# A two-layer graph network on one core: fillers at norm 2 and in attention's last pair, single heads, a 15th unit before the experts, GpSimd adds, and another order in relation 1

## The chip, the cores and the metric

The kernel runs on one core of a Trainium2 chip. The metric is the device time of one execution in microseconds (us). Five sequencers work at once: PE (TensorE, matrix products), DVE (VectorE), ACT (ScalarE), POOL (GpSimd) and SP (SyncE, which here issues the weights' DMAs). They wait for one another only by semaphores, and each takes its instructions strictly in the order in which the program lists them.

## The reference

There are 625 nodes of D = 1024 float32 features and 10,625 edges. Cut to what matters:

```python
xn = layernorm(x)
x = x + gnn0(xn) + mix0(xn)         # support[src]*w summed by dst; linear attention
x = x + ffn0(layernorm(x))          # 16 experts, top 2, capacity 98, F=1408, and a shared MLP
xn = layernorm(x)
x = x + gnn1(xn) + mix1(xn)
x = x + ffn1(layernorm(x))          # 8 small experts, a shared MLP

def ffn0(x):
    probs = softmax(x @ router_w + router_b); vals, idx = top_k(probs, 2)
    # each expert gets its rows (at most 98), mlp(h) = silu(h@wg)*(h@wu) @ wd
    return x + mlp(x, sw_gate, sw_up, sw_down) + gathered.reshape(N, 2, d).sum(1)

def gnn1(x):                        # u: relations r = 0..7
    u = x @ root + bias + sum_r mean_r(x[src] -> dst) @ weight[r]
    z = concat([u, x]) @ w_gate + b_gate
    return tanh(u) * z + x * (1 - z)

def mix1(x):                        # 16 heads of 64, 256 features
    q, k, v = split(x @ Wqkv + bqkv)
    f = lambda t: exp(t @ omega - 0.5 * sum(t*t))
    out = f(q) @ (f(k).T @ v) / (f(q) @ sum(f(k)) + 1e-6)
    return out @ Wout + bout
```

## The kernel before

**Tiles and products.** Nodes lie in T = 5 tiles of TP = 125. To keep float32's precision each operand is split in a high part (a copy to fp32r, on ACT, `a_high`) and a low part (the operand minus the high part, on DVE, `v_low` and `lo_of`, line 270), and each product is three matrix products, high by high, low by high, high by low (`mm3`, line 234). TensorE is therefore fed by two steps on two engines: a weight comes by SP's DMA in a raw tile, ACT makes the high part, DVE the low one.

**Order.** No scheduler sets the order. For each engine a program is written out (`tensor`, `scalar`, `vector`, `gpsimd`, `sync`), made of functions with the prefixes t_, a_, v_, p_ and s_ for the five. What must be in the same order on several engines (the weights' chunks) is in a list `W` that `weights` fills; PSUM's eight banks are given out in turn by `ps.take`, and a product waits for the step that emptied its bank.

**Stages** (us in the profiled execution): norm 1, features and linear attention mix0 to 200; the adjacency matrix and its spread to 314 (`t_adjacency`, `t_spread`); norm 2 to about 327; the experts to 1330; norm 3 to 1344; the relations to 1816; attention to 2060; the window to about 2290; then gate, norm 4 and the small ffn.

**Norm 2.** `v_spread` adds the aggregated products to x and takes statistics; tiles 0 to 2 are normalized and turned (transposed on TensorE, `t_turn_norm`, line 1236) during the spread, tiles 3 and 4 after it in `t_layernorm`. A turned tile leaves PSUM as T_h by ACT (`a_turned_norm`) and T_l by DVE (`v_turned_norm`). The space of T is shared, and `T_free` says from when it may be written. Then comes routing: `t_route` makes the logits from rw, in two halves of the nodes.

**Experts.** The shared MLP is cut into units (`t_unit`: a gate, an up or a down block, about 7 us of TensorE each), 11 during routing, three more before the experts, and then one with each of experts 0 to 10 and with expert 15. Ten indirect DMAs of POOL (`scr_ei<-xn,sdi`, line 2228) scatter the rows to the experts' places; `xin<-scr_ei` reads one expert's back, and `t_enter` transposes them. At the end ten gathers bring the experts' outputs yg back, and `v_combine` weights and adds two of them for each tile on DVE, among the last units; `v_add_x` adds the last units' products, with the statistics of norm 3.

**Relations.** Each relation's product is made in blocks by sums and differences of quarters of the matrix B and of T (`v_block_mixed`, `v_mixed`, and their low parts `v_block_low`). `v_last` makes one more of the sums.

**Attention.** Eight pairs of heads. For a pair p, z (k or q, `v_z`) is split in both heads at once, then `t_keys`, `t_queries`, `t_values`, `t_turn_values` and `t_attend` follow for s = 0, 1; features are made by ACT and split by DVE (kp, qp); kw is the product of keys and values, rt the divisor, whose reciprocal `v_over` takes 628 columns.

**Window.** 200 slots in five blocks of 40 (KD = 8 chunks of k by T = 5 tiles): root and Wout in two halves each, then one block of the gate. A slot is one `mm3`. Between slots SUM0 = 14 and SUM1 = 178 lie the 96 sums of gathered rows (`t_sum`): for each, POOL gathers 128 rows of y (`gr`, line 2345), ACT scales them (`gh`, line 2308) and makes a 0/1 matrix (`gs`), DVE makes the low part (`gl`, line 266), TensorE makes four products, and the buffers (six) come free for another gather. `a_part` and `v_part` split the attention's output oT into oh and ol in the first block.

## Time and profile before

| | us |
|---|---|
| three runs: lowest, median, highest | 2518.45, 2518.72, 2530.13 |
| the profiled execution, its own time | 2521.97 |
| its span, first to last instruction | 2520.1 |
| TensorE busy | 2438.6 (97%) |
| DVE busy | 1811.3 (72%) |
| ACT busy | 1421.7 (56%) |
| POOL busy | 653.3 (26%) |
| chain that ended last | PE 84%, DVE 8%, DMA 3%, issue 2%, ACT 2%, POOL 1% |
| mean granted TensorE clock | 0.989 of full speed |

A share of busy time is a mean over stages with different limits, so an edit is read at its place: what TensorE waits for there, and what stands ahead of it on the engine waited for. DMA-issuing instructions aren't counted as busy. In timelines a row may be several instructions of one kind ("x16"), with the time that TensorE stood ahead of it and what ended that in brackets.

### The profile page before, as it was taken

The numbers are of one execution on the slowest core, as the hardware profiler recorded it, in microseconds if no ns is written. First come the engines' busy times: TensorE is split into PE (matmuls) and PEld (weight loads), VectorE is DVE, ScalarE is ACT, GpSimd is POOL, SyncE is SP. The second block draws the span as 40 slices with busy tenths as digits, with TensorE's granted clock in tenths as the row PEclk, the third lists the DMA queues.
The fourth block names the chain that finished last, engine by engine and source line by source line (L and its number), as shares of the span: only waits on it lengthen the run. The fifth ranks groups of instructions, "written<-read, shape, count | busy, mean of one in ns | idle before, by whom it ended". The sixth has DMA issues, their size and how long they took to land.

```text
span 2520.1 us, 32144 instructions
## 1 busy us (share of the span) xinstructions
PE 2438.6 (97%) x12692; PEld 2019.6 (80%) x12692; DVE 1811.3 (72%) x2006; ACT 1421.7 (56%) x1890; POOL 653.3 (26%) x538
## 2 busy tenths in 40 slices
PE   7999998999999999999998999999999979999999
PEld 6978788777777777777787777777899977777797
DVE  7449664888878888788868876556567778887453
ACT  5327432777677767777733344443377758884131
POOL 5758204434431000000021005442000016556000
PEclk9999999999999999999999999999999999999999
DMA  6334026999999899999974344445211138884212
GB/s 176 78 100 129 1 80 216 332 337 334 350 352 350 336 335 336 360 390 374 354 216 158 104 155 137 118 135 162 91 44 56 54 114 277 285 275 142 92 56 74
DMA packets 128013, 508.14 MB, mean 202 GB/s; under 512 B 26892, under 2 KB 44697, under 8 KB 101240
## 3 DMA queue, kind: packets, MB, share of 16 engines
q1 hardware_dynamic: 78440, 418.00, 46.2%
q0 software_dynamic: 34928, 74.92, 10.5%
q10 hardware_dynamic: 14496, 13.17, 1.6%
q8 instruction: 101, 1.65, 0.3%
q14 instruction: 48, 0.39, 0.0%
HBM read 458.93 MB, written 46.88 MB: 201 GB/s over the span
## 4 chain that ended last, share of the span: by engine, by line
PE 84%; DVE 8%; DMA 3%; issue 2%; ACT 2%; POOL 1%; SPq 0%; DVEq 0%; ACTq 0%
PE ps L231 83%; DVE od L262 2%; DMA scr_ei<-xn,sdi 1%; DVE Aw L258 1%; DVE x L258 1%; DMA wk<-in_Wk 1%; DVE ua L258 1%; PE ps L2025 1%; PE ps L1236 1%; DMA gr<-scr_y,gidx 1%; POOL scr_ei L2228 1%; DVE zq_l L270 0%; PE ps L1993 0%; DVE ws_l L270 0%; ACT gh L2308 0%
## 5 line engine op out<-in xcount | busy, mean ns | idle before, releaser
L270 DVE TENSOR_TENSOR pr_l<-pr,hs 128x1408 fp32r<-128x1408 f32 (+1 forms) x455 | 645.5, 1444 | 137.3 <-ACT hs L793 134.5
L793 ACT ACTIVATE hs<-pr 128x1408 fp32r<-128x1408 f32 (+1 forms) x455 | 559.0, 1242 | 205.3 <-PE ps L231 164.5
L793 ACT ACTIVATE ws_h<-wr 128x1024 fp32r<-128x1024 f32 (+1 forms) x105 | 110.2, 1051 | 206.7 <-PE ps L231 199.6
L270 DVE TENSOR_TENSOR ws_l<-wr,ws_h 128x1024 fp32r<-128x1024 f32 (+1 forms) x103 | 129.8, 1261 | 115.4 <-ACT ws_h L793 115.2
L231 PE MATMUL ps<-hs,xe_h 128*98 128x512 f32 (+1 forms) x768 | 205.5, 376 | 0.0
L231 PE MATMUL ps<-pr_l,xe_h 128*98 128x512 f32 (+1 forms) x768 | 205.0, 375 | 0.0
L231 PE MATMUL ps<-hs,xe_l 128*98 128x512 f32 (+1 forms) x768 | 204.6, 374 | 0.0
L2234 POOL DMA_DIRECT2D xin<-scr_ei x16 | 9.4, 590 | 581.1 <-PE ps L1993 550.3
L231 PEld LDWEIGHTS ps<-pr_l,xe_h 128*98 128x98 f32 x768 | 124.8, 163 | 38.8 <-DVE pr_l L270 0.9
L231 PEld LDWEIGHTS ps<-hs,xe_l 128*98 128x98 f32 x768 | 125.0, 163 | 38.2
L231 PEld LDWEIGHTS ps<-hs,xe_h 128*98 128x98 f32 x768 | 123.8, 163 | 36.7
L2345 POOL DMA_INDIRECT gr<-scr_y,gidx x96 | 125.0, 1302 | 100.2 <-PE ps L231 78.9
L3058 POOL DMA_INDIRECT wrow<-scr_inv,gdst x96 | 110.3, 1149 | 154.7 <-DVE B_l L270 93.1
L1205 POOL DMA_INDIRECT scr_edges<-dat,idx x85 | 141.7, 1667 | 25.9 <-issue 25.9
L270 DVE TENSOR_TENSOR T_l<-T,bh 128x1024 fp32r<-128x1024 f32 x64 | 78.3, 1225 | 70.1 <-ACT bh L2856 70.1
L266 DVE SCALAR_TENSOR_TENSOR gl<-gr,gw,gh 128x1024 fp32r<-128x1024 f32 x96 | 120.6, 1279 | 10.5 <-ACT gh L2308 10.3
L231 PE MATMUL ps<-ws_h,T_h 128*125 128x512 f32 x320 | 127.3, 398 | 0.0
L231 PE MATMUL ps<-ws_h,T_l 128*125 128x512 f32 x320 | 126.6, 396 | 0.0
L231 PE MATMUL ps<-ws_l,T_h 128*125 128x512 f32 x320 | 126.6, 396 | 0.0
L2308 ACT ACTIVATE gh<-gr,gw 128x1024 fp32r<-128x1024 f32 x96 | 109.7, 1143 | 25.1 <-DMA gr<-scr_y,gidx 18.5
L231 PE MATMUL ps<-T_h,ws_h 128*128 128x314 f32 x528 | 121.1, 309 | 0.7 <-DVE ws_l L270 0.7
L1195 POOL DMA_INDIRECT scr_wedges<-dat,widx x85 | 109.7, 1291 | 45.8 <-issue 27.5
(476 smaller groups left out, 6263.6 us busy)
## 6 DMA issues: line engine op xcount, KB each, us to landing
pr<-in_wg SPq DMA_DIRECT2D x64, 1408.0 KB, 7.9
pr<-in_wu SPq DMA_DIRECT2D x64, 1408.0 KB, 8.4
pr<-in_wd SPq DMA_DIRECT2D x80, 1024.0 KB, 6.8
B<-in_rel SPq DMA_DIRECT2D x64, 512.0 KB, 3.4
scr_y<-y SPq DMA_DIRECT2D x45, 448.0 KB
pr<-in_wd_last SPq DMA_DIRECT2D x16, 512.0 KB, 5.2
wr<-in_Wqkv SPq DMA_DIRECT2D x16, 512.0 KB, 5.4
wr<-in_gate SPq DMA_DIRECT2D x16, 512.0 KB, 3.4
```

The source lines that it names most:

```text
L231: return e.matmul(out, l, r, start=start, stop=stop, skip_group_check=True)
L258: return e.tensor_tensor(out, x, y, op)
L262: return e.tensor_scalar(out, x, s1, s2, op0) if op1 is None else e.tensor_scalar(out, x, s1, s2, op0, op1)
L266: return e.scalar_tensor_tensor(out=out, in0=x, scalar=s, in1=y, op0=op0, op1=op1)
L270: return e.tensor_tensor(lo, src, hi.bitcast(F32), ALU.subtract)
L793: q.e.activation(c.hi, c.at, ACT.Copy).then_inc(*self.s("high").up(c.key))
L1195: e.indirect_dma_start(self.d_wedges, to, m["dat"][0:TP, 4 * c:4 * c + 4], None).then_inc(*self.landed("weighted_edges").up(c))
L1205: q.e.indirect_dma_start(self.d_edges, to, self.m["dat2"][0:TP, 4 * c:4 * c + 4], None).then_inc(*self.landed("edges").up(c))
L1236: ins = e.transpose(ps.one(bs[k // 4], 128, (k % 4) * TP, TP), buf[t][:, k * 128:(k + 1) * 128], self.ident[0:TP, 0:TP])
L2308: q.e.activation(m[f"gh{c % NH}"], m[f"gr{c % NR}"], ACT.Copy, scale=m["gw"][:, c:c + 1]).then_inc(*self.s("rows_high").up(c))
L2345: e.indirect_dma_start(m[f"gr{c % NR}"], None, self.d_y[:, :], of).then_inc(*self.landed(f"rows{c % NR}").up(c))
L3058: e.indirect_dma_start(m["wrow"][:, c * 8:(c + 1) * 8], None, self.d_inv[:, :], of).then_inc(*self.landed("row_weights").up(c))
```

## The change

Seven places, in the order of the program:

1. Spread: aw_h and aw_l lie elsewhere (U, and over data of mix 0, so that DVE's aw_l waits `mix0_sums`), and `T_free` for norm 2 waits only for A_low. The low parts of om and rw and T_l of tiles 0 to 2 are made by DVE ahead of the last adds.
2. Norm 2: `t_first` makes the products of rw and of the first shared gate block for tiles 0 to 2 before the turns of tiles 3 and 4, the rest behind them.
3. Experts: 15 units come ahead instead of 14, so that expert 10 has none, and SP's load of `("wg", 0, 4)` waits for the last scatter to have landed.
4. Norm 3: ACT scales the last four gathered rows, GpSimd adds them, DVE adds and takes statistics of tiles as they come.
5. Relation 1: the order of DVE.
6. Attention: z is split by single heads, each in turn.
7. Last pair and window: `t_last_pair` weaves 20 slots of root in; SUM0 is 30; the parts are split as they are finished.

```diff
-SUM0, SUM1 = 14, 178
+SUM0, SUM1 = 30, 178
...
-        pair("aw", R2 + 12576, 3140)
+        at("aw_h", U, 3140, F32R)
+        at("aw_l", R3 + 23040, 3140, F32R)
...
-        for i in range(11, 14):
+        for i in range(11, 15):
...
-            if e < E0 - 5 or e == E0 - 1:
+            if e < E0 - 6 or e == E0 - 1:
...
+            if c.key == ("wg", 0, 4):
+                q.wait_ge(self.landed("placed"), 2 * T - 1)
...
+    def t_first(self, q, L, keys):
+
+        outs = {key: self.t_pair(q, key) for key in keys}
+        for i in range(2):
+            q.wait_ge(*self.ps.done(("ln", L, (2, T - 1)[i]), 1, "low"))
+            both, _ = self.t_chunk(q, keys[0])
+            for k in range(KD):
+                for j in range(2):
+                    ins = mm(q.e, outs[keys[0]][i], both[:, k * 128:(k + 1) * 128], self.Tk(k)[i][j], k == 0 and j == 0, k == KD - 1 and j == 1)
...
+            hi, lo = self.t_chunk(q, keys[1])
+            for k in range(KD):
+                c = slice(k * 128, (k + 1) * 128)
+                ins = mm3(q.e, [outs[keys[1]][i]], (hi[:, c], lo[:, c]), [self.Tk(k)[i]], k == 0, k == KD - 1)
...
+                for t in range(3, T):
+                    self.t_turn_norm(q, L, t)
...
-            q.wait_ge(self.s("aggregated"), T - 1)
+            q.wait_ge(self.s("A_low"), T - 1)
...
+            q.wait_ge(self.s("mix0_sums"), ("num", 1, T - 1))
...
+            if t == T - 1:
+                self.v_low(q, ("om", 0))
+                self.v_low(q, ("rw", 0))
+                self.v_no_nodes(q, 1)
+                for s in range(3):
+                    self.v_turned_norm(q, 1, s)
...
+            e.activation(y, y, ACT.Copy, scale=m["vs"][0:TP, i:i + 1]).then_inc(*self.s("gathered_weighted").up(i))
...
-        for t in range(3, T):
-            self.v_combine(q, t)
...
+            tt(e, x, x, m[f"yg{i % 7}"][0:TP, :], ALU.add).then_inc(*self.s("combined_by_gpsimd").up(i))
...
+        self.t_last_pair(q)
+
+    def t_last_pair(self, q):
+
+        ps = self.ps
+        self.slot_banks = [1, 2, 3, 4, 5]
...
+        self.t_values(q, 7, 0)
+        self.t_values(q, 7, 1)
+        self.t_root(q, 0, (0,))
...
+        self.t_turn_values(q, 7, 0)
+        self.t_root(q, 0, (1,))
...
+        self.t_turn_values(q, 7, 1)
...
+        self.t_attend(q, 7, 0)
+        self.t_root(q, 1, (0,))
...
+        self.t_attend(q, 7, 1)
+        self.t_root(q, 1, (1,))
...
-        e.tensor_copy(m[nm + "_h"], et).then_inc(*self.s("z_high").up((nm, p)))
-        q.wait_ge(self.s("z_high"), (nm, p))
-        lo_of(e, m[nm + "_l"], et, m[nm + "_h"]).then_inc(*self.s("z_low").up((nm, p)))
+        for s in range(2):
+            c = slice(s * NT, (s + 1) * NT)
...
+            e.tensor_copy(m[nm + "_h"][:, c], et[:, c]).then_inc(*self.s("z_high").up((nm, p, s)))
+            q.wait_ge(self.s("z_high"), (nm, p, s))
+            lo_of(e, m[nm + "_l"][:, c], et[:, c], m[nm + "_h"][:, c]).then_inc(*self.s("z_low").up((nm, p, s)))
...
-                    self.v_last(q)
-        self.v_block_mixed(q, 1, "T1", 0)
+        for j in range(2):
+            self.v_block_mixed(q, 1, "T1", j)
+            self.v_block_low(q, 1, j)
         self.v_mixed(q, 1)
-        self.v_block_low(q, 1, 0)
-        self.v_block_mixed(q, 1, "T1", 1)
-        self.v_block_low(q, 1, 1)
+        self.v_last(q)
```

Three places of the order that is the result. The first is GpSimd ahead of norm 3: yg are the experts' gathered rows, ws_l a weight of relation 0. Before:

```order
L2245 DMA yg_239<-scr_eo,sgi 125x1024
L2245 DMA yg_240<-scr_eo,sgi 125x1024
L2245 DMA yg_241<-scr_eo,sgi 125x1024
L270 TENSOR_TENSOR ws_l<-wr_60,ws_h 128x1024
L2252 DMA scr_xn<-lnx_84 112x1024
L2252 DMA scr_xn<-lnx_84 13x1024
```

and of the change:

```order
L2288 DMA yg_237<-scr_eo,sgi 125x1024
L2288 DMA yg_238<-scr_eo,sgi 125x1024
L2288 DMA yg_239<-scr_eo,sgi 125x1024
L258 TENSOR_TENSOR x<-x,yg_243 125x1024
L258 TENSOR_TENSOR x<-x,yg_237 125x1024
L258 TENSOR_TENSOR x<-x,yg_238 125x1024
L258 TENSOR_TENSOR x<-x,yg_239 125x1024
L270 TENSOR_TENSOR ws_l<-wr_60,ws_h 128x1024
L2302 DMA scr_xn<-lnx_84 112x1024
```

Four adds now stand between the last gather and the weight's low part and the stores of the normalized rows.

The second is DVE at the start of relation 1; T_0, T_1, B_0 and B_1 are the two blocks of the matrices, s the sums of T. Before:

```order
L258 TENSOR_TENSOR x<-x,row 125x1024 x5
L258 TENSOR_TENSOR s_162<-T_h 128x500
L258 TENSOR_TENSOR s_162<-s_162,T_l 128x500 x2
L258 TENSOR_TENSOR T_0_173<-B_0_183,B_0_169 128x1024
L270 TENSOR_TENSOR s_l<-s_156,s_h 128x1000
L270 TENSOR_TENSOR B_0_l<-B_0_169,bh_202 128x1024
L258 TENSOR_TENSOR T_1_175<-B_1_185,B_1_171 128x1024
L270 TENSOR_TENSOR B_1_l<-B_1_171,bh_324 128x1024
```

and of the change:

```order
L258 TENSOR_TENSOR x<-x,row 125x1024 x5
L258 TENSOR_TENSOR T_0_173<-B_0_183,B_0_169 128x1024
L270 TENSOR_TENSOR B_0_l<-B_0_169,bh_202 128x1024
L258 TENSOR_TENSOR T_1_175<-B_1_185,B_1_171 128x1024
L270 TENSOR_TENSOR B_1_l<-B_1_171,bh_324 128x1024
L270 TENSOR_TENSOR s_l<-s_156,s_h 128x1000
L258 TENSOR_TENSOR s_162<-T_h 128x500
L258 TENSOR_TENSOR s_162<-s_162,T_l 128x500 x2
L270 TENSOR_TENSOR s_l<-s_159,s_h 128x1000
```

Both low parts of B now come ahead of all low parts of sums, and the two rows of s_162 (`v_last`) behind the first of these.

The third is DVE in attention's last pair; rt is the divisor, kw the keys' product, ol the low parts of the attention's output, gl the low part of a gathered row. Before:

```order
L270 TENSOR_TENSOR kp_l<-et_258,kp_h 125x1280
L2683 RECIPROCAL rt<-rt 128x628
L258 TENSOR_TENSOR oT<-oT,rt 128x628
L270 TENSOR_TENSOR qp_l<-et_322,qp_h 128x1256
L270 TENSOR_TENSOR ws_l<-wr_62,ws_h 128x1024
L270 TENSOR_TENSOR kw_l<-ps,kw_h 128x256
L262 TENSOR_SCALAR rt<-ps 64x628
L270 TENSOR_TENSOR kw_l<-ps,kw_h 128x256
L262 TENSOR_SCALAR rt<-ps 64x628
L2683 RECIPROCAL rt<-rt 128x628
L258 TENSOR_TENSOR oT<-oT,rt 128x628
L270 TENSOR_TENSOR ol_267<-oT,oh_266 128x628
```

and of the change:

```order
L270 TENSOR_TENSOR ws_l<-wr_62,ws_h 128x1024
L270 TENSOR_TENSOR qp_l<-et_320,qp_h 128x1256
L2792 RECIPROCAL rt<-rt 128x628
L258 TENSOR_TENSOR oT<-oT,rt 128x628
L270 TENSOR_TENSOR kw_l<-ps,kw_h 128x256
L270 TENSOR_TENSOR ol_273<-oT,oh_272 128x628
L270 TENSOR_TENSOR ol_275<-oT,oh_274 128x628
L270 TENSOR_TENSOR kw_l<-ps,kw_h 128x256
L270 TENSOR_TENSOR ol_265<-oT,oh_264 128x628
L262 TENSOR_SCALAR rt<-ps 64x628
L270 TENSOR_TENSOR ol_267<-oT,oh_266 128x628
L270 TENSOR_TENSOR ws_l<-wr_60,ws_h 128x1024
```

The reciprocal of pair 6 now stands behind qp_l and the root's low part, and the ol's are made between the steps of the last pair instead of behind it.

## Rows read from the trace of the kernel before

**Rows 1.** The page's first part: busy us, share of the span, instructions.

```profile
PE 2438.6 (97%) x12692; PEld 2019.6 (80%) x12692; DVE 1811.3 (72%) x2006; ACT 1421.7 (56%) x1890; POOL 653.3 (26%) x538
```

**Rows 2.** TensorE's waits: who, for what; us in total, times, longest.

```profile
PE ps L1236 <- ACT lnx L1254: 9.1, 3, 7.1
...
PE ps L1993 <- DMA xin<-scr_ei: 7.7, 1, 7.7
...
PE ps L231 <- DVE zq_l L270: 6.8, 8, 3.9
...
PE ps L231 <- DVE kw_l L270: 5.7, 2, 4.4
...
PE ps L231 <- DVE B_l L270: 2.9, 1, 2.9
```

**Rows 3.** Stretches: us, busy by engine, TensorE clock, DMA share, GB/s.

```profile
319.40:322.80 3.40, 3.40 (x17) 3.40 (x18) 3.04 (x6) 1.31 (x3) 0.00 (x0) 0.53 0.00 0
...
427.30:431.70 4.40, 4.40 (x20) 4.40 (x21) 1.75 (x3) 2.15 (x3) 3.48 (x4) 0.50 0.09 2
...
1052.00:1098.00 46.00, 46.00 (x221) 34.07 (x219) 40.71 (x35) 36.42 (x37) 0.55 (x1) 1.00 0.97 383
...
1404.00:1412.00 8.00, 6.49 (x16) 5.09 (x17) 8.00 (x8) 1.51 (x2) 0.00 (x0) 0.57 0.83 270
...
2041.00:2093.00 52.00, 38.78 (x180) 31.81 (x178) 38.91 (x36) 32.39 (x58) 16.86 (x15) 0.90 0.63 197
...
2093.00:2315.00 222.00, 216.13 (x930) 166.44 (x930) 194.08 (x204) 180.80 (x292) 131.66 (x100) 1.00 0.78 254
```

**Rows 4.** Norm 2: timelines of PE and DVE, and the stretch behind.

```profile
319.36 3.46 PE L1236 MATMUL ps<-cst,xn 125*128 125x125 f32 x16 [5.21 <-DVE xn L262]
...
321.92 1.26 DVE L270 TENSOR_TENSOR T_l<-ps,T_h 128x500 fp32r<-128x500 f32 x2 [0.36 <-ACT T_h L1291]
...
322.80:334.60 11.80, 11.80 (x85) 11.80 (x84) 4.97 (x6) 4.53 (x6) 0.00 (x0) 1.00 0.29 90
```

**Rows 5.** Tile scr_ei: its DMAs, durations in ns, issue times, landing.

```profile
L2234 POOL DMA_DIRECT2D xin<-scr_ei x16: 552/604/646, 421.3 to 1148.1; - x16
...
L2228 POOL DMA_INDIRECT scr_ei<-xn,sdi x10: 1177/1230/2090, 373.1 to 388.4; - x10
...
DMA to landing us min/median/max: 5.7/7.5/32.6
```

**Rows 6.** Timelines: DVE before norm 3; GpSimd's adds in the gate.

```profile
1317.03 5.45 DVE L266 SCALAR_TENSOR_TENSOR x<-yg,vs,x 125x1024 f32<-125x1024 f32 x4
...
1335.09 0.16 DVE L266 SCALAR_TENSOR_TENSOR shift<-mv,nrm 125x3 f32<-125x3 f32 x1
...
2299.81 3.27 POOL L258 TENSOR_TENSOR x<-x,tb 125x1024 f32<-125x1024 f32 x1
...
2319.85 2.40 POOL L258 TENSOR_TENSOR x<-x,tb 125x1024 f32<-125x1024 f32 x1
```

**Rows 7.** DVE's timeline in relation 1: the last T_l.

```profile
1420.81 1.23 DVE L270 TENSOR_TENSOR T_l<-T,bh 128x1024 fp32r<-128x1024 f32 x1 [0.65 <-ACT bh L2856]
```

**Rows 8.** DVE's timeline at the first pair's queries.

```profile
1827.89 1.47 DVE L270 TENSOR_TENSOR zq_l<-et,zq_h 128x1256 fp32r<-128x1256 f32 x1
```

**Rows 9.** Last pair and window: timelines, a group, gathers' landing.

```profile
2045.51 4.07 DVE L2683 RECIPROCAL rt<-rt 128x628 f32<-128x628 f32 x1
...
2076.25 0.76 PE L231 MATMUL ps<-gh,gs 128*125 128x512 f32 x1 [5.39 <-DVE gl L266]
...
2288.25 0.39 PE L231 MATMUL ps<-ws_h,T_h 128*125 128x512 f32 x1
...
2288.95 0.39 PE L231 MATMUL ps<-gh,gs 128*125 128x512 f32 x1
...
L266 DVE SCALAR_TENSOR_TENSOR gl<-gr,gw,gh 128x1024 fp32r<-128x1024 f32 x88 | 110.4, 1278 | 6.2 <-ACT gh L2308 6.1
...
DMA to landing us min/median/max: 4.6/5.7/8.6
```

195 lines of the change are left out of this document (134 added, 61 removed).

## The prediction

> **What bounds the kernel now.** I read the page's busy times first, then TensorE's waits, then the clock by stretch, and last the timelines at the places that the diff touches. TensorE is busy for 2438.6 of 2520.1 us [rows 1]. So the change can give back at most the 81.5 us in which TensorE stands, and what the lowered clock costs after such a stand; an edit on another engine counts only where TensorE waits for that engine. The largest waits are for the normalized rows of norm 3 (9.1 us), the rows scattered for expert 0 (7.7), the products kw of attention's last pair (5.7), the low parts zq_l of the pairs (6.8 in eight) and the low part of relation 1's first matrix (2.9) [rows 2]. The reader is to see a second price in the stretches: after a wait of some us the granted clock stands near 0.5 (1.2 of 2.4 GHz) for 3 to 7 us, and work that took 4.4 us there takes half as long elsewhere [rows 3]. I charge each long wait with both.
>
> **Norm 2.** Before, TensorE stands 5.21 us for xn and then makes 16 transposes in 3.46 us [rows 4] at a clock of 0.53, which costs 3.4 x 0.47 = 1.6 us [rows 3]. Together 6.8. The change puts the routing's and the first unit's products of tiles 0 to 2 (40 of the 80 short products that took 11.80 us behind the transposes [rows 4], so 5.9 us) ahead of these transposes. They need no xn of tiles 3 and 4, so the stand at 314.1 is filled to 320.0, about when xn is there. The transposes then take 1.7 us at the full clock. What is late next is the low part of tile 4: ACT's copies and DVE's subtractions (1.26 a tile, and the copies about as long) follow the transposes, two tiles one behind the other [rows 4], to about 324.0, a new stand of 2.3 us. If the clock falls in it, another 1.8 goes. Net 6.8 - 2.3 = 4.5 without the drop, 2.7 with it. **+3.5** (2.7 to 4.7), as I cannot tell from the rows which it is.
> Its side is that aw_l of the spread now lies over data that mix 0 still reads, so DVE's first subtraction starts about 0.5 us later than it did: **-0.5** (-1 to 0).
>
> **Expert 0's rows.** The last of ten scatters is issued at 388.4 and takes 32.6 us to land, the read-back is issued at 421.3 and takes about 6 (5.7 is its least) [rows 5]. TensorE stands for 7.7 us [rows 2], then runs 4.4 us at 0.50, which costs 2.2 [rows 3]. The change puts one more unit, 7.0 us of TensorE, between routing and this point, and SyncE's third load of expert 0 waits for the scatters. The unit alone takes 7.0 of the 7.7; norm 2's 3.5 us moves both sides alike. A load of 1.4 MB less beside the scatter's last 8 us should bring the landing forward by some us. **+9.9**: stand and drop both go. If the load gives nothing, 0.7 us is left: still above 9. If the scatter lands later instead, the bound is 5.
> The unit is taken from expert 10, so five experts in a row have no unit. In such an expert TensorE is busy 46.00 of 46.00 us beside DMA engines at 0.97 [rows 3]: no spare transfer time, but four of them in a row hold without a stand, so the fifth is costed at 0. Its cover is the ring of loaded weights; if that ran dry, each of its us would count in full.
>
> **Norm 3.** Before, DVE weights and adds the last four gathered rows (5.45 us) and reaches the shift at 1335.09 [rows 6]; TensorE waits 7.1 us there [rows 2]. The change has ACT scale these rows and GpSimd add them. A GpSimd add of this form takes 2.40 us when DVE stands and 3.27 when DVE works beside it on two SBUF tiles (ua and xnk) [rows 6]. Four of them one behind the other from 1317.5 are 9.6 or 13.1 us, to 1327.1 or 1330.6. In that time DVE adds PSUM halves of tiles 0 to 2 and takes statistics, and needs tile 3 after the second add, tile 4 after the fourth. At 2.40 DVE is done with tile 4 (0.62 a half) and its queue at 1328.2, against 1328.6 before (5.45 and twice 3.1 for adds and statistics of half 0, from 1317.03). It then has two more statistics (0.7 us each) ahead of and behind the root, as they are no longer made early. The shift stays at about 1335.2, so **0**. The other end is 3.27 an add, which moves it back by 2.5 to 3. All of DVE's operations there read one SBUF operand, so I take 2.40. The Trainium skill says, in "SBUF — State Buffer", section "Who interferes with whom", that DVE with at most one SBUF input does not contend with GpSimd, while with two it meets GpSimd's reads; by that rule the sum stays 31, and by the slower row it would be 28. The trace agrees where it can: the 3.27 lies beside an operation of two SBUF tiles.
> GpSimd's subtraction for relation 0, queued behind the adds, ends some 3.4 us later, still before norm 3 is over: 0.
>
> **Relation 1.** TensorE stands 2.9 us [rows 2] until B_l is made and runs at 0.57 to 1412, which costs about 3.1 [rows 3]. The change makes the same DVE operations in another order: T1, B_l, T1, B_l, then the sums' low parts. B_l ends near 1402.3, just when TensorE wants it. But DVE works without a pause, so TensorE, now at full clock, meets steps 2, 3 and 4 too early, by about 1.4, 1.7 and 0.6 us. The last T_l here ended at 1422.04 [rows 7], and would end near 1420.2. **+2** (-1 to +3).
>
> **Attention, heads split singly.** A single step makes both heads' high part, then 1.47 us of low part [rows 8], and TensorE stands 3.9 us at the start and (6.8 - 3.9) / 7 = 0.42 in each further pair [rows 2]. With halves (0.74 us of low part) the first head is ready 1.1 us after its data instead of 2.3. The seven waits go: **+2.9**. At the start the wait falls to about 1.1, and with it goes most of a clock drop that I charge like the one of 4.4 us behind expert 0's wait, at 2.2: 2.8 and 2.2. ACT's features of the first keys are next in line and late by some 2 us, so I take **+3.0** (2 to 4.5) of the 5.
>
> **Last pair, root and window.** In the stretch from 2041 to 2093 TensorE works 38.8 of 52 us at a clock of 0.90 [rows 3]; its largest stands there are 4.4 and 1.3 (kw_l, [rows 2]) and 5.39 (the first sum, [rows 9]). The reciprocal of pair 6 (4.07 us, [rows 9]) stands on DVE ahead of kw_l. The change moves 20 of the window's 200 slots into these waits, puts the reciprocal behind qp_l and spreads the subtractions ol over the pair. So TensorE should run nearly without a stand for 24.9 us of pair and slots, to 2066.3, and ten more slots of 0.70 (three products, [rows 9]) to slot 30 at 2073.3. Here the first sum comes, where it came at 2076.25 and slot 14 before. The later gathers still wait for the last ol, about 2072, and land near 2077.6, so the third sum waits some 2 us, to 2080.0. From there are left 145 slots x 0.705 + 94 sums x 0.93 (four products) = 189.6 us, so slot 178 is reached at 2269.6 if TensorE sets the pace. It was at 2286.2, 2.8 us ahead of the last sum. But the sums come closer: 2.01 us of TensorE instead of the (2288.95 - 2076.25) / 95 = 2.24 of before. DVE needs 1.28 a sum [rows 9], and the adds and low parts beside it: 194 of 222 us before [rows 3], about 188 of 193.5 now; in four weight blocks it has more than TensorE. I put 6 us of waits here (3 to 14). **+10.5** (4 to 17), the largest term and the least sure.
>
> **Sum.** 3.5 - 0.5 + 9.9 + 0 + 2 + 3 + 2.9 + 10.5 = 31.3 us. The page's execution took 2521.97 us, so 2490.7; it stands 3.25 above the median of the runs, 2518.72, and against that I forecast **2488**. All low ends together give 12, all high ends 43. The norm 4, the ffn and everything before 270 us are the same, 0.
>
> **Rivals.**
> 1. The window is set by DVE, ACT and the gathers. For it: DVE's 188 of 193.5 us and a DMA share of 0.78 in it already [rows 3]. Against: TensorE stood only 5.9 of 222 us in this stretch [rows 3] while DVE had 13% free. Then the slots moved out buy nothing and the sums keep 2.24 us: 31.3 - 10.5 = 20.8, so 2498, to 2505 if pair and window wait for each other.
> 2. Nothing new stands. The two clock drops of norm 2 and relation 1 stay away and the window loses 2 instead of 6: 43 us, 2476. Against: four places above where the next operand is late by arithmetic.
> 3. The change doesn't do what it says at expert 0. The scatters' landing moves with the unit, because the unit's own weights add traffic, and TensorE stands again for over 2 us and loses the clock: 5 to 8 us less, 2494; norm 3 behind GpSimd at 3.27 each adds 3: 2497.
> 4. Slower. Place: the loop of six gathered buffers in the window. Its parts are a landing of 5.7 us (8.6 the longest, [rows 9]), ACT's copy 1.1, DVE's 1.3, the sum 0.9 and about 1.4 of hand-overs, 10.4 us, and six run at once, so 1.73 a sum. If the closer sums lengthen the landing, the loop sets the pace. The other terms' 20.8 us are used up when 95 sums take 212.7 + 20.8, that is 2.46 us each, a loop of 14.7 and a landing of 10.0; at 2.6 us a sum the kernel takes 2532. The longest landing of all is under that, and transfers ran at 0.97 without a stand elsewhere [rows 3], so this is unlikely.
>
> **How the numbers follow.** Forecast, with its parts as above, 2480 to 2495: 0.55. Rival 1: 0.20. Rival 2: 0.12. Rival 3: 0.09. Rival 4: 0.04. A change under 0.5% (12.6 us) cannot be told from none here. Faster by more: all but rival 4 and the low corner of rival 1, 0.91; within 0.5%: 0.06; slower: 0.03. The range of 2470 to 2504 takes in rivals 2 and 3 and most of rival 1.
>
> **What would show it.** TensorE's waits should no longer list xin over 1 us nor zq_l over 1.5; norm 2 should show a wait for T_l of about 2 us instead of xn's 5.2; norm 3's 7.1 should stay within 1 us; B_l should be replaced by three short waits for T_l; kw_l should be under 1, and slot 178 should come about 10 us earlier beyond what the start of the last pair gains. GpSimd's four adds should last 2.4 each. The forecast is wrong if TensorE's idle time in the window rises by over 15 us, if the read-back for expert 0 is late again, or if a wait for weights appears in experts 10 to 14.

## The result, and the profile after

| | before | changed |
|---|---|---|
| median of 19 runs each | 2516.09 us | 2504.32 us |
| lowest to highest | 2512.39 to 2530.13 | 2498.68 to 2514.35 |
| ratio of the times, 95% interval | | 0.9948 (0.9936 to 0.9960) |
| the profiled execution, its own time | 2521.97 | 2505.01 |
| its span | 2520.1 | 2502.9 |
| mean granted TensorE clock | 0.989 | 0.995 |

The change is faster by 0.52% (0.40 to 0.64%) by the ratio, which is 13 us; between the two medians lie 11.8 us (0.47%). Forecast were 2488 and a range of 2470 to 2504. The sign is right, but the time lies 16.3 us above the forecast and 0.3 us above the range, and 12 to 13 us came where the sum had 31.3. Both profiles are compared below against each other: there the gain is 17.2 us of span, since the profiled execution of before was itself 6 us above its median.

The page's first part, changed kernel:

```profile
PE 2430.6 (97%) x12692; PEld 2008.8 (80%) x12692; DVE 1810.3 (72%) x2034; ACT 1425.5 (57%) x1894; POOL 662.8 (26%) x542
```

TensorE makes the same 12692 products and is busy 8 us less than in [rows 1], as it is at its full clock for more of the time; the other 9 of the 17.2 us are stands that are gone. TensorE's waits, changed kernel (who, for what; us in total, times, longest):

```profile
PE ps L1262 <- ACT lnx L1280: 9.2, 3, 7.3
...
PE ps L231 <- DVE gl L266: 7.9, 10, 2.1
...
PE ps L231 <- DVE T_l L270: 6.2, 5, 2.3
PE ps L231 <- DVE ua L258: 5.9, 7, 1.6
PE ps L231 <- issue: 5.5, 9, 0.7
...
PE ps L231 <- DVE zq_l L270: 1.3, 1, 1.3
```

Against [rows 2]: xin (7.7), kw_l (5.7) and B_l (2.9) are gone, and zq_l is down from 6.8 to 1.3. In their place stand T_l (0.8 us before; now norm 2 and relation 1), "issue" nine times (seven of them one and the same wait in the pairs), and ua (0.4 before), DVE's adds of finished sums to the result, which empty the PSUM banks for the next ones. gl, the low part of a gathered row, had 7.3 us before too, but in four waits, of which one of 5.4 stood ahead of the first sum; now it has 7.9 in ten.

The stretches that answer to [rows 3], and the sums' stretch (us, busy by engine, TensorE clock, DMA share, GB/s):

```profile
325.40:328.80 3.40, 3.35 (x14) 3.35 (x15) 0.00 (x0) 0.00 (x0) 0.00 (x0) 0.56 0.02 5
409.00:417.00 8.00, 8.00 (x50) 7.48 (x49) 4.53 (x6) 1.06 (x1) 5.92 (x6) 1.00 0.91 311
1052.00:1098.00 46.00, 46.00 (x224) 34.66 (x223) 40.50 (x34) 36.29 (x37) 0.56 (x1) 1.00 0.97 379
...
2026.00:2055.00 29.00, 28.34 (x151) 23.98 (x150) 24.71 (x23) 19.05 (x34) 4.07 (x4) 1.00 0.68 184
2057.00:2272.00 215.00, 199.41 (x823) 148.43 (x822) 185.17 (x192) 180.23 (x295) 126.88 (x104) 1.00 0.83 272
```

The reader is to see three things. Around the read-back of expert 0, issued at 409.6, TensorE is full at full clock. The last pair, which stood at 38.8 of 52 us and a clock of 0.90 before, now has 28.34 of 29 us at 1.00, so the forecast for its own stands was right. And the stretch that holds the 96 sums is no shorter than it was. The same view of the kernel before, over the same 96 sums:

```profile
2076.00:2289.00 213.00, 208.41 (x867) 159.70 (x868) 186.28 (x194) 182.51 (x299) 125.70 (x103) 0.99 0.84 277
```

TensorE has 9.0 us less work there than before (199.41 against 208.41: sixteen slots have moved out), and DVE and ACT have nearly what they had (185.17 and 186.28; 180.23 and 182.51). First to last sum took 212.7 us [rows 9] and takes 214.3 (2057.42 to 2271.73). TensorE's stands went from 4.6 to 15.6 us. What was taken out of the window came back in it as waiting. The other traces say that this is no accident of two of them. In three with the window of before (before, before_again, window_before) first to last sum takes 210.3 to 212.7 us and TensorE stands 2.9 to 4.3 of them; in seven with the changed window untouched (after, after_again, third_after, z_together, no_hold, units_14, norm3_split) it takes 210.3 to 214.3 us and TensorE stands 11.9 to 15.6.

**Norm 2.** One row of PE's timeline stands for what is left of it, where [rows 4] had 5.21 for xn:

```profile
325.45 0.41 PE L231 MATMUL ps<-T_h,ws_h 128*128 128x314 f32 x1 [2.30 <-DVE T_l L270]
```

The stand of 2.3 us "to about 324" came as forecast, and in this execution the clock fell behind it (0.56 in 325.4 to 328.8).

**Expert 0's rows.** Tile scr_ei, changed kernel (durations in ns, issue times):

```profile
L2277 POOL DMA_DIRECT2D xin<-scr_ei x16: 552/604/646, 409.6 to 1137.3; - x16
L2271 POOL DMA_INDIRECT scr_ei<-xn,sdi x10: 1177/1229/2082, 372.2 to 387.6; - x10
```

From the last scatter's issue to the read-back's are 22.0 us, where [rows 5] have 32.9. TensorE does not stand for xin at all.

**Norm 3.** GpSimd's adds, and DVE's waits for them, changed kernel:

```profile
1306.80 9.85 POOL L258 TENSOR_TENSOR x<-x,yg 125x1024 f32<-125x1024 f32 x4 [10.22 <-ACT yg L2141]
```
```profile
1311.79 0.69 DVE L258 TENSOR_TENSOR x<-ps,x 125x512 f32<-125x512 f32 x1 [1.50 <-POOL x L258]
1316.68 1.49 DVE L258 TENSOR_TENSOR x<-ps,x 125x512 f32<-125x512 f32 x2 [4.20 <-POOL x L258]
```

Four adds in 9.85 us are 2.46 each: the fast one of the two prices in [rows 6], as the forecast took it. TensorE's wait for lnx is 7.3 us against 7.1.

**Relation 1 and attention's start.** PE's timelines at both places, changed kernel:

```profile
1401.67 0.50 PE L231 MATMUL ps<-bh,s_h 128*125 128x512 f32 x1 [1.28 <-DVE T_l L270]
1406.21 0.50 PE L231 MATMUL ps<-bh,s_h 128*125 128x512 f32 x1 [1.51 <-DVE T_l L270]
1409.59 0.49 PE L231 MATMUL ps<-bh,s_h 128*125 128x512 f32 x1 [0.30 <-DVE T_l L270]
...
1814.17 0.56 PE L231 MATMUL ps<-zq_h,om_h 128*128 128x314 f32 x2 [1.26 <-DVE zq_l L270]
...
1816.81 0.38 PE L231 MATMUL ps<-om_h,zk_h 128*125 128x256 f32 x1 [0.62 <-ACT kp_h L2637]
```

Three short waits for T_l where forecast were 1.4, 1.7 and 0.6; 1.26 for zq_l where forecast was 1.1, and the first keys' features next in line.

**The pairs.** Each of seven pairs has this wait, once:

```profile
1874.84 0.53 PE L231 MATMUL ps<-qp_h,kw_h 128*128 128x314 f32 x2 [0.72 <-issue]
```

The wait of 0.42 for zq_l is gone from every pair, and 0.72 stands 2.7 us further on. A pair took 29.40 us and takes 29.40. The row names no releaser, so I looked at what TensorE's product may overwrite: it takes the PSUM banks of the next pair's first keys, which ACT must have read. ACT's timeline there:

```profile
1872.39 0.38 ACT L2767 ACTIVATE kw_h<-ps 128x256 fp32r<-128x256 f32 x1 [0.28 <-PE ps L2599]
1872.67 0.60 ACT L2636 ACTIVATE et<-ps 125x512 f32<-125x512 f32 x1
1873.15 0.61 ACT L2637 ACTIVATE kp_h<-ps 125x512 fp32r<-125x512 f32 x1
1873.63 0.62 ACT L2636 ACTIVATE et<-ps 125x512 f32<-125x512 f32 x1
1874.10 0.63 ACT L2637 ACTIVATE kp_h<-ps 125x512 fp32r<-125x512 f32 x1
```

The second kp_h, which frees the second bank, ends at 1874.73, and TensorE starts at 1874.84. The two rows that answer to these in the kernel before, at the first of its seven waits:

```profile
1860.44 0.63 ACT L2545 ACTIVATE kp_h<-ps 125x512 fp32r<-125x512 f32 x1
1861.17 0.53 PE L231 MATMUL ps<-qp_h,kw_h 128*128 128x314 f32 x2
```

There, too, TensorE's product starts 0.10 us behind the end of this kp_h (1861.07), though no wait is listed at it, since TensorE had stood for zq_l shortly before. So the same chain on ACT set the time of this product in both kernels. The theory can be tested by a run (keys_then_kw below).

### The profile page after: what moved, and what is told of

The parts are those of the page before. It is cut to its first block, busy times and chain, and to the rows that moved or that the text cites. A ratio compares the mean times of both kernels' runs of the same rounds, so it can differ in the third digit from the quotient of the medians.

```text
span 2502.9 us, 32203 instructions
## 1 busy us (share of the span) xinstructions
PE 2430.6 (97%) x12692; PEld 2008.8 (80%) x12692; DVE 1810.3 (72%) x2034; ACT 1425.5 (57%) x1894; POOL 662.8 (26%) x542
## 4 chain that ended last, share of the span: by engine, by line
PE 85%; DVE 8%; DMA 2%; ACT 2%; issue 2%; POOL 0%; SPq 0%; DVEq 0%; ACTq 0%; POOLq 0%
PE ps L231 83%; DVE od L262 2%; DMA gr<-scr_y,gidx 1%; DVE ua L258 1%; DVE x L258 1%; DVE Aw L258 1%; DVE gl L266 1%; DVE ws_l L270 1%; PE ps L2065 1%; DMA pr<-in_wu 1%; DMA wk<-in_Wk 0%; ACT ws_h L795 0%; PE ps L1262 0%; ACT gh L2360 0%; PE ps L2033 0%
## 5 line engine op out<-in xcount | busy, mean ns | idle before, releaser
L795 ACT ACTIVATE ws_h<-wr 128x1024 fp32r<-128x1024 f32 (+1 forms) x105 | 110.0, 1051 | 202.8 <-PE ps L231 198.4
L270 DVE TENSOR_TENSOR T_l<-T,bh 128x1024 fp32r<-128x1024 f32 x64 | 78.2, 1225 | 68.8 <-ACT bh L2978 63.4
L2360 ACT ACTIVATE gh<-gr,gw 128x1024 fp32r<-128x1024 f32 x96 | 109.7, 1142 | 30.6 <-DMA gr<-scr_y,gidx 17.2
```

The lines of the kernel that those rows point to most:

```text
L270: return e.tensor_tensor(lo, src, hi.bitcast(F32), ALU.subtract)
L795: q.e.activation(c.hi, c.at, ACT.Copy).then_inc(*self.s("high").up(c.key))
L2360: q.e.activation(m[f"gh{c % NH}"], m[f"gr{c % NR}"], ACT.Copy, scale=m["gw"][:, c:c + 1]).then_inc(*self.s("rows_high").up(c))
```

## The experiments

Medians are of the runs named, on four further occasions and three chips, each beside runs of the kernel before on the same chip; so ratios to before are what is compared from batch to batch. The interval of a ratio is 0.0010 to 0.0023 either way (3 to 6 us), and much of what follows therefore rests on the profiles. One length from them serves throughout: from the first reciprocal of attention (row rt, L2792) to the last sum (gl). It holds six of the seven waits between pairs, the last pair and the window, and leaves out what happens ahead of it. It is 418.7 us in the kernel before (1870.27 to 2288.95) and 417.2 in the changed one (1854.55 to 2271.73); I call it **the length**. The sum of the prediction had some 13 us of gain inside it. It varies by itself: the seven traces with the changed window untouched, named above, give 413.2 to 417.2.

| run | edit against the changed kernel | median us (runs) | ratio to before | the length, us |
|---|---|---|---|---|
| before_again | the kernel before | 2524.07 (1) | | 418.4 |
| after_again | none | 2502.33 (6) | 0.9945 | 414.9 |
| third_after | none | 2501.01 (8) | 0.9951 | 414.7 |
| z_together | both heads split in one step again | 2503.74 (9) | 0.9962 | 414.0 |
| window_before | last pair, root and window as before | 2506.34 (8) | 0.9968 | 417.3 |
| no_hold | SyncE's load doesn't wait for the scatters | 2502.48 (6) | 0.9953 | 415.6 |
| units_14 | 14 units ahead of the experts, and no hold | 2508.57 (12) | 0.9961 | 413.2 |
| keys_then_kw | ACT makes a key chunk ahead of kw_h | 2499.25 (6) | 0.9935 | 411.1 |
| norm3_split | GpSimd adds tile 3 only | 2498.18 (6) | 0.9936 | 414.1 |
| light_dve | less low part in the window | 2492.83 (4) | 0.9912 | 411.4 |
| light_dve_2 | the same | 2497.61 (6) | 0.9933 | 410.3 |
| light_act | less high part in the window | 2496.47 (4) | 0.9937 | 412.6 |
| light_both | both | 2491.84 (6) | 0.9915 | 407.3 |
| gr5 | five gather buffers for six | 2512.15 (10) | 0.9987 | 429.2 |
| combined | keys_then_kw and norm3_split | 2498.74 (6) | 0.9937 | 413.8 |
| combined_va | the same, and the values moved | 2501.15 (5) | 0.9947 | 411.7 |

**The kernel before, once more.**

> The kernel before, unchanged. The page's execution of it took 2521.97 us, 5.9 above the median of its 19 runs (2516.09), while the page of the changed kernel fits its own median. Theory: the landing of expert 0's scatters differs from run to run, so here TensorE's wait for xin is 2 to 4 us and not 7.7, and the execution takes 2514 to 2517. Rival: the wait is 7 to 8 us again, and the 5 us lie elsewhere (the start of the kernel, or the window).

One profile, 2524.07 us. Its wait for the rows of expert 0:

```profile
PE ps L1993 <- DMA xin<-scr_ei: 8.0, 1, 8.0
```

So the theory (a wait of 2 to 4 us here) missed, and the rival's wait came: the stand of 7.7 us was no accident of the one trace. But both profiles of this kernel (2521.97 and 2524.07) lie above what most of its runs take (median 2514.24 of this occasion), and neither need show the middle run. That matters below.

**Heads split together again.** The edit puts `v_z` and the waits for it back (cut):

```
-q.wait_ge(self.s("z_low"), ("zk", p, s))
+q.wait_ge(self.s("z_low"), ("zk", p))
-q.wait_ge(self.s("z_low"), ("zq", p, s))
+q.wait_ge(self.s("z_low"), ("zq", p))
...
```

> The changed kernel with both heads' z split in one step again. Theory: in each further pair TensorE's wait for zq_l only gave way to one for the bank that ACT's second chunk of key features empties, so the period of a pair stays 29.40 us and only the start of attention is lost: 3 us slower than the changed kernel, with the seven waits back to 0.42 for zq_l. Rival (the prediction's): each pair is longer by 0.4 us as well, 6 us slower.

Its TensorE waits:

```profile
PE ps L231 <- DVE zq_l L270: 6.8, 8, 3.9
```

That is the row of [rows 2] to the digit: 3.9 at the start and seven of 0.42. A pair takes 29.40 us with these waits, as it takes 29.40 with the 0.72 in their stead. So the split is worth the start of attention alone (3.85 against 1.26 + 0.62 + 0.40), and nothing in the seven pairs. The ratio, 0.9962 (0.9950 to 0.9974), is 0.0011 to 0.0017 above the three of the changed kernel (0.9945, 0.9948, 0.9951), some 3 to 4 us, which agrees within its width.

**Last pair, root and window as before.** `t_attention`, `t_window`, `a_attention`, `v_attention`, `a_part`, `a_rows` and the two window functions of ACT and DVE are taken from the kernel before, with its slots:

```
-SUM0, SUM1 = 30, 178
+SUM0, SUM1 = 14, 178
```

> The changed kernel with attention's last pair and the window as before (no root slots in the last pair, SUM0 = 14). Theory: the moved slots were given back by a tighter window, so this is only 1 to 3 us slower than the changed kernel; the sums start some 3 us later, and TensorE's waits among them fall from about 13 us back to 4. Rival (the prediction's): 9 to 11 us slower.

Measured: 2506.34 us, 0.9968 (0.9955 to 0.9981), so by the ratios 4 to 6 us slower than the changed kernel, and 4 us slower than no_hold of the same occasion; the intervals overlap. The length is 417.3 against 414.7 to 417.2. All three old waits are back: 1.15 for kvf, 4.40 and 1.08 for kw_l, and 5.38 for gl at the first sum, 12.0 us together. Yet the kernel loses only 4 to 6, more than the theory had and half of what the prediction had. The traces say where: from the first reciprocal to the first sum are 206.9 us here and 202.8 to 202.9 in the changed kernel's three, so 4 us are saved ahead of the sums. From first to last sum are 210.3 us here and 211.8 to 214.3 there. The last pair does shed its stands, and among the sums nothing of the expected gain is left.

**Without SyncE's hold.**

```
-            if c.key == ("wg", 0, 4):
-                q.wait_ge(self.landed("placed"), 2 * T - 1)
```

> The changed kernel without SyncE's wait for the scatters ahead of expert 0's third load. Theory: the 15th unit alone hides the landing, so the time is the same within 1 us, and the last scatter lands 27 to 33 us after its issue, ahead of TensorE's arrival. Rival: the held load is what brings the landing forward, and without it TensorE waits 2 us or more for xin and loses the clock behind it, 4 us slower.

2502.48 us, 0.9953 (0.9937 to 0.9968): the same. The read-back is issued at 411.5, 26.8 us behind the last scatter, and TensorE does not stand for it. The load that waits for the scatters buys nothing that can be measured; the fifteenth unit hides the landing.

**Fourteen units.**

```
-        for i in range(11, 15):
+        for i in range(11, 14):
-        u = 15
+        u = 14
-            if e < E0 - 6 or e == E0 - 1:
+            if e < E0 - 5 or e == E0 - 1:
```

> The changed kernel with 14 units ahead of the experts and no held load, as before. Theory: in the profile TensorE waits 7 to 8 us for xin and loses 2 more behind it, so the profiled execution is about 10 us longer than the changed kernel's; in the executions that are only timed the scatters land sooner, and the median is only 4 to 6 us longer. Rival (the prediction's): both are 9 to 10 us longer.

2508.57 us over 12 runs, and they don't scatter about it: five lie from 2498.4 to 2502.3, seven from 2506.8 to 2514.9. The profiled run is the fastest of all, 2498.41, and shows no stand for xin: its read-back is issued at 406.6, 20.2 us behind the last scatter at 386.4. So the expected stand of 7 to 8 us in the profile did not come: where the landing is early, fourteen units do as well as fifteen. (In both profiles of before it was later, 32.9 and 33.8 us behind the last scatter.) With the fifteenth unit the time is 2 to 6 us lower (by the ratios, 0.9953 and 0.9945 against 0.9961, 2 to 4; by the medians 6), not 9.9, though the intervals overlap. The 17 runs of the kernel before beside these fall apart in the same way: nine lie from 2511.0 to 2515.5 and eight from 2518.5 to 2526.7. That the long runs are those of a late landing is what the two profiles of before make likely; none of the seven was profiled.

**One key chunk ahead of kw_h.** ACT makes the first chunk of the next pair's key features, then kw_h, then the rest:

```
-            self.a_feature(q, "k", p, 0)
+            self.a_feature(q, "k", p, 0, (lambda: self.a_kw(q, p - 1, 1)) if p else None)
...
-            self.a_kw(q, p, 1)
```

> The changed kernel with ACT making the first chunk of the next pair's key features ahead of kw's high part. Theory: TensorE's 0.72 us a pair is the wait for the bank that the second chunk of key features empties, on ACT's chain behind the turn of the values; ACT idles 0.28 us there, so the chain gets shorter by about 0.3 us, the period of a pair falls from 29.40 to about 29.1, and the kernel is 2 us faster. Rival: the wait is TensorE's own or for kw, and the period stays at 29.40 or grows.

The wait in each pair shrinks and now has its name:

```profile
1876.55 0.53 PE L231 MATMUL ps<-qp_h,kw_h 128*128 128x314 f32 x2 [0.50 <-ACT kp_h L2637]
```

The period falls from 29.40 to 29.17, and the run takes 2499.25 us, 0.9935 (0.9915 to 0.9954): 3 us less than after_again beside it, of which 7 x 0.23 = 1.6 are the pairs. The intervals of the two overlap, so the evidence is the period and the releaser that the row names, and by them the theory of the banks stands.

**GpSimd with one tile only.** DVE weights and adds tile 4 itself:

```
-        for i in range(6, 2 * T):
+        for i in range(6, 8):
...
-                    if t > 2:
+                    if t == 3:
+                        self.v_combine(q, 4)
```

> The changed kernel with only tile 3's two gathered rows scaled by ACT and added by GpSimd, and tile 4's weighted and added by DVE, which waited 5.7 us for GpSimd there. Theory: DVE gets on 2 to 3 us sooner and norm 3's wait falls from 7.3 to 4 or 5 us, though DVE's two additions and GpSimd's, with two SBUF inputs each, hold one another up by 1 to 2 us; the kernel is 1 to 3 us faster. Rival: the statistics behind TensorE's last product set the end, and the time stays.

DVE's and GpSimd's timelines of this run:

```profile
1308.56 4.00 DVE L266 SCALAR_TENSOR_TENSOR x<-yg,vs,x 125x1024 f32<-125x1024 f32 x2
```
```profile
1305.15 4.95 POOL L258 TENSOR_TENSOR x<-x,yg 125x1024 f32<-125x1024 f32 x2 [12.33 <-ACT yg L2142]
1311.45 3.39 POOL L270 TENSOR_TENSOR ws_l<-wr,ws_h 128x1024 fp32r<-128x1024 f32 x1 [1.35 <-ACT ws_h L795]
```

Norm 3's wait falls from 7.3 to 5.5 us, since DVE works 4.0 us where it stood 1.5 and 4.2, and does not wait for the fourth add. Even so DVE's two operations of two SBUF tiles cost 2.0 us each beside GpSimd, where one alone in the same run takes 1.28, and GpSimd's ws_l 3.39 where it took 2.40. The Trainium skill's "SBUF — State Buffer", section "Who interferes with whom", has this: DVE with two SBUF inputs meets GpSimd's reads, and with one, outside the two-port performance modes, it doesn't. By that rule the changed kernel's own four adds, beside DVE operations with one SBUF operand, should stay at 2.4, as they do, though DVE stood for 5.7 of their 9.85 us. The kernel takes 2498.18 us, 0.9936 (0.9913 to 0.9959).

**Less for DVE in the window, less for ACT, and both.** These kernels leave out part of the work: for the sixteen matrices of root and Wout the low part (`v_low`), the high part (`a_high`) or both are made for 64 of 1024 columns. In `v_low`, and alike in `a_high`:

```
+                if c.key[0] in ("root", "Wout"):
+                    lo, at, hi = (z[:, 0:64] for z in (lo, at, hi))
```

> This kernel leaves out work: the low parts of the sixteen window matrices of root and Wout are made for 64 of 1024 columns only, so DVE has 16 x 1.1 = some 17 us less in the window (of the 202 it is busy there with the changed kernel); everything else is the changed kernel, 2502 to 2504. Theory (a chain with engines in fixed order and a look-ahead of two rows sets the pace; it is opened by gathers that land late, and is not DVE's total load alone): part of the 17 us comes back, 3 to 6 us, so 2497 to 2501. Rival, DVE's load alone sets the window: TensorE's stands in it fall by nearly all of 13 us, 2490 to 2493. Rival, the loop of gathered buffers: nothing comes back, within 1.5 us of the changed kernel.

> This kernel leaves out work: the high parts of the same sixteen window matrices are copied for 64 of 1024 columns only, so ACT has 16 x 1.0 = 15 us less in the window and the rest is the changed kernel. Theory (the coupled chain, ACT is the first link behind a landed gather): 2 to 5 us back, 2498 to 2501. Rival, DVE's load alone: nothing back, 2502 to 2504. Rival, the loop of gathered buffers: at most 1 us.

The first of these, light_dve, came out at 2492.83 us, a larger gain than the theory gave and inside the rival's 2490 to 2493. So it was run again beside the changed kernel, and once more with both parts lightened:

> The changed kernel once more, as the measure for the runs beside it: 2501 to 2505.

> The kernel of light_dve again (it leaves out the low parts of the sixteen window matrices of root and Wout but for 64 of 1024 columns). Theory (coupled chain, DVE and ACT both full): 4 to 6 us under the changed kernel of the same chip. Rival (DVE's load alone sets the window): 9 us or more under it.

> Leaves out both the high and the low parts of the sixteen window matrices of root and Wout but for 64 of 1024 columns: 17 us of DVE and 15 us of ACT. Theory: the two add up, since each link of the chain gets shorter; TensorE's stands in the window halve and the gathers that land late are left, 7 to 10 us under the changed kernel. Rival, DVE's load alone: the same as light_dve_2 within 1.5 us. Rival, the gathers alone: under 3 us.

| | median us | against third_after | the length | sum to sum, us |
|---|---|---|---|---|
| third_after | 2501.01 | | 414.7 | 2.229 |
| light_dve_2 | 2497.61 | -3.4 | 410.3 | 2.184 |
| light_both | 2491.84 | -9.2 | 407.3 | 2.153 |

The sums' stretch of the three, in the same order (third_after, light_dve_2, light_both):

```profile
2054.00:2267.00 213.00, 199.25 (x825) 149.38 (x824) 185.07 (x192) 180.74 (x295) 127.47 (x104) 1.00 0.84 275
```
```profile
2058.00:2266.00 208.00, 197.66 (x822) 149.14 (x821) 173.11 (x191) 179.58 (x295) 120.33 (x103) 1.00 0.85 281
```
```profile
2053.00:2258.00 205.00, 196.38 (x822) 149.70 (x821) 173.00 (x191) 171.37 (x295) 121.51 (x103) 1.00 0.86 285
```

DVE gives up 12 us of this stretch, and by the last column 4.3 come back (95 x 0.045); ACT gives up 8 more, and 2.9 come back. With DVE at 173 of 205 us (84%) and ACT at 84% TensorE still stands 8.6 us. Against the rival of DVE's load speak the stands: they fall from 13.8 to 10.3 us where DVE gives up 12. light_both lies 5.8 us under light_dve_2, which fits a chain whose links add up, but the runs of the two overlap (2492.85 to 2500.93 and 2490.12 to 2498.01), and what ACT's link is worth is less sure than what DVE's is. The first light_dve, 5 us lower than its repeat and with the ratio of light_both (0.9912 and 0.9915), differs in its clock: its four runs show 0.996 to 0.998, the six of the repeat 0.993 to 0.997, in the mean two thousandths less, which is an estimate of 5 us at this length of run. The lengths of the two (411.4 and 410.3) do not differ in its favour. light_act came out at 2496.47, under the 2498 to 2501 of its theory; by the ratio (0.9937 against 0.9945 to 0.9951) it gains 2 to 3.5 us, as expected, but neither that nor its length of 412.6, beside 413.2 to 417.2 without the edit, stands clear of what varies by itself.

**Five gather buffers.**

```
-NR, NH, NS = 6, 3, 6
+NR, NH, NS = 5, 3, 6
```

> The changed kernel with five gather buffers instead of six, so each gather is issued one sum later. Theory (the loop is slack most of the time and only the landings of 8 us and more open a stand): with 5 x 2.26 = 11.3 us for a loop that needs 10.4 to 13.3, more gathers become late and TensorE stands 4 to 12 us longer, 2506 to 2516. Rival, the loop sets the pace already (what my fourth rival said): every sum takes 6/5 as long, 2.7 us, so 95 x 0.45 = 43 us more, 2545. Rival, DVE's load alone sets it: within 2 us of the changed kernel.

ACT's waits for landed gathers, the changed kernel and gr5 (us until that came, times):

```profile
  DMA gr<-scr_y,gidx: 17.2, 9
```
```profile
  DMA gr<-scr_y,gidx: 39.1, 29
```

2512.15 us, 0.9987 (0.9977 to 0.9998), 8 to 11 more than the changed kernel; the length grows by 12 to 14.5. A sum now takes 2.382 us, and five of them 11.9. As ACT waited for a gather at 29 of 96 sums only, the loop of a buffer takes no more than these 11.9 us on the mean; I had put 10.4 for it. With six buffers a round is 6 x 2.256 = 13.5 us, so some 1.6 us or more are to spare on the mean, and the landings vary by more (4.4 to 8.4 in gr5, with a median of 5.6). One gather in ten lands too late in the changed kernel (9 of 96), one in three with five buffers. But late gathers are nothing that the change brought. The same row of the kernel before:

```profile
  DMA gr<-scr_y,gidx: 18.5, 16
```

There ACT stood for gathers more often and as long, and TensorE had little to wait for. Seven buffers were not tried.

The chain of waits in the changed kernel, from 2093 to 2272, tells the same from the other side (by line; then one of its episodes):

```profile
by line: PE ps L231 50.5%; DMA gr<-scr_y,gidx 14.0%; DVE gl L266 8.1%; issue 7.0%; DVE ua L258 6.0%; ACT gh L2360 5.8%; DVE ws_l L270 2.6%; DVE x L258 2.6%; ACT ws_h L795 1.6%; ACT go L2351 1.2%; DVEq L258 0.4%; ACT gs L2354 0.3%; DVEq L72 
...
2092.90 3.04 PE ps L231 x13
2096.20 7.95 DMA gr<-scr_y,gidx
2104.17 1.16 ACT gh L2360
2105.57 0.98 issue
2106.56 0.69 DVE ua L258
```

Half of the window's time runs through something other than TensorE, and the episode shown starts at a gather that took 7.95 us. The kernel before, in the same stretch:

```profile
by line: PE ps L231 74.8%; DVE ua L258 5.7%; issue 4.9%; DMA gr<-scr_y,gidx 4.8%; DVE gl L266 3.8%; ACT gh L2308 2.6%; DVE ws_l L270 1.9%; ACT go L2299 0.7%; ACT ws_h L793 0.5%; DVEq L258 0.3%; ACT gs L2302 0.3%; DVEq L72 0.1%; DVEq L2322 0
```

There three quarters ran through TensorE (78.2% in window_before), and in after_again it is again 50.6%, with 8.9% for the gathers.

**Two mends together.**

> Three edits to the changed kernel together: the next pair's first key chunk ahead of kw_h on ACT (was 3 us alone), the high part of the values moved behind the first key features on ACT (0.74 us that stands ahead of the released chunk), and only tile 3 of norm 3 left to GpSimd (1.7 us in the profile alone). Theory: the seven waits of 0.50 that are left in the pairs go too, so the period falls from 29.40 to about 28.7, 5 us in all, and with norm 3's 1.7: 2502.3 - 6.7 = 2495 to 2497. Rival, the waits in the pairs move to the next link (kvf behind the features): 3 + 1.7, 2497.5 to 2499. Rival, the window takes back what comes early, as it did with the last pair: 2499 to 2502.

> The edits of keys_then_kw and norm3_split together, without the move of the values. Period 29.17 as alone, norm 3's wait 5.5: 1.6 + 1.7 = 3.3 us in the profile and, as the window starts earlier and waits no more than before, 3 to 6 us under the changed kernel, 2497 to 2500. Rival, the window or the clock takes it back: under 1.5 us.

combined_va adds this to keys_then_kw and norm3_split, and the same on DVE:

```
+            if p:
+                self.a_values(q, p)
...
             self.a_out(q, p, 0)
-            self.a_values(q, p + 1)
```

With the values moved a pair takes 29.30 us, not the 28.7 of the theory and more than the 29.17 without: a miss, and at 2501.15 us (0.9947) the kernel is no faster than the changed one. In its trace TensorE still waits 0.51 us for kp_h in each pair, and ACT, with the values out of its way, stands 0.81 us for TensorE ahead of the first of these chunks; why the period grows is open. combined takes 2498.74 us, 0.9937 (0.9916 to 0.9958); its pairs take 29.18 and norm 3 waits 5.5 us, as in the two runs alone, so the parts are there, 3.3 us in the profile. By its ratio it is no faster than either mend alone (0.9935 and 0.9936). keys_then_kw, norm3_split and combined lie 2 to 4 us under the changed kernel by the ratios; with these intervals none can be told from the others, nor surely from the changed kernel.

## Why the prediction was right where it was, and wrong where it was not

- **What bounds the kernel; norm 2 (+3.5), aw_l (-0.5), expert 0 (+9.9).** In the two profiles the start of norm 3's products (ahead of them the wait for lnx) moved from 1336.67 to 1326.07, so 10.6 us came of 12.9; norm 2's stand fell from 5.2 to 2.3 us with a clock drop behind it, aw_l's grew from 0.43 to 1.07, expert 0's stand and its drop are gone. The steps held. What failed is the step from one profiled execution to the median: I took the stand of 7.7 us for that of every run. The profile of units_14 has none with the same fourteen units, and its times and those of before fall in two groups, so over the runs the term is worth 2 to 6, not 9.9. The same holds for the base: I subtracted only 3.25 us for the profiled execution's place, and with 19 runs it stands 5.9 above the median.
- **Experts 10 to 14 (0) and norm 3 (0).** Right. TensorE is busy 46.00 of 46.00 us in the stretch shown, 1052 to 1098, and has no wait over 0.25 us from 950 to 1320; GpSimd's adds took the fast price. That tile 4 could be done sooner in another way was not foreseen; norm3_split's wait is 1.7 us shorter there.
- **Relation 1 (+2).** Right: 2.92 us of B_l and the drop behind it against 1.28 + 1.51 + 0.30 for T_l. Across it the lead over the kernel before grows from 10.6 to 12.7 us.
- **Attention's start (+3.0).** Right: 3.9 against 1.26 + 0.62 + 0.40 with no drop, and z_together puts it back. Here the lead grows from 12.7 to 15.9.
- **The seven pairs (+2.9).** Wrong: 0. The failed step is "the seven waits go". They went, but I did not ask what is late next, as I did at the start. The next product waits for PSUM banks that ACT frees at the end of kw_h, et, kp_h, et, kp_h (2.34 us in one row), and this chain was ready no sooner than before: it starts at the turned values (L2507, now L2599), and from these to the product are 2.86 us in both kernels (1858.31 to 1861.17, 1842.58 to 1845.44). keys_then_kw, which only reorders this chain, shortens the period.
- **Last pair, root and window (+10.5).** Wrong, 1.5 in the two profiles, some 3 to 4 by the length of the unchanged repeats, and 4 to 6 by window_before. The timelines up to the third sum came as written: 28.34 of 29 us in the last pair, the first sum 18.8 us earlier, a wait of 2.12 at the third. The failed step is "6 us of waits here", after "if TensorE sets the pace". TensorE's stands are 15.6 us, and a sum takes 2.256 us where I had 2.01 and the pace of before was 2.239. My first rival said just this, "the slots moved out buy nothing and the sums keep 2.24 us", and named 2498 for it; I gave it 0.20 because TensorE had stood only 5.9 of 222 us in that stretch. That was the wrong reading. TensorE stood little because it had 9 us more to do there. That the other engines and the gathers had no such room is what the runs point to: DVE was busy 87% and ACT 86% (186.28 and 182.51 of 213 us), beside gathers that land between 4.6 and 8.6 us in a ring of six buffers; light_dve_2 and light_both give 3.4 and 9.2 us back, and gr5 costs 8 to 11. How much of the limit each link has, and how much lies in the order of DVE's work, no run here shows.
- **The rivals.** Rival 1 held for the window. Its 2498 to 2505 took in the time partly by luck, as the pairs' 2.9 us and the place of the profiled execution are in that time too. Rival 2 (nothing new stands) did not. Rival 3's landing did not move later: 22.0 us against 32.9. Rival 4's loop counts, as gr5 shows, but it takes up to 11.9 us where a round of six buffers has 13.5, so it doesn't set the pace of every sum.
- **The sum.** In the profiles 31.3 were forecast and 17.2 came. Up to norm 3's products 10.6 came of 12.9: the clock fell in norm 2 (0.8), and 0.9 were lost in the first 90 us, where nothing was changed. From there to attention's first reciprocal 5.1 came of 5.4 (533.6 us against 528.5; relation 1, attention's start and the first of the seven waits). In the length 1.5 came of 13.0, and behind the last sum nothing moved (231.2 us in both). So the missing 14 us are 9.0 of the window, 2.9 of the pairs and 2.3 at the start. The forecast is off by 2 us more, since it took 3.25 us off for the profiled execution's place and that of the changed kernel lies only 0.7 above its median. The high ends of the terms as written add up to 42 and not to 43, which changes nothing.

## What to carry to other kernels

Moving work out of a stretch pays only as far as the stretch was bound by the engine that did the work: compare the busy time of every engine in it, and the round of its buffers, with the time per step before you count the slots as gained. When a wait goes, name the next operand and the next bank that its successor needs, at each place where the wait stood and not only at the first. And before a stand in one profiled execution is priced, set that execution beside the other runs, since a transfer may land late in some and in time in others.
